# Down projection of a pre-norm transformer layer: 2x2 block products with seven multiplications, weights cast in DRAM

## The reference

```python
x = x + attention(layernorm(x)) @ Wo + bo        # 32 heads, 8 KV heads, head size 64
h = layernorm(x)
Wg, Wu, Wd = ((w - 128) * scale[:, None] for w, scale in
              ((gate_w, gate_scale), (up_w, up_scale), (down_w, down_scale)))
y = silu(h @ Wg.T) * (h @ Wu.T)                  # 8192 wide
out = x + y @ Wd.T                               # back to 2048
```

## Time and profile before

| | us |
|---|---|
| median of 3 runs | 2027.4 (2023.74 to 2028.51) |
| the profiled execution, own time | 2026.54 |
| its span on the slowest core | 2025.0 |
| spans of the other cores | 2020.3 to 2024.1 |
| PE busy | 1975.2 (98% of the span) |
| DVE busy | 1038.9 (51%) |
| ACT busy | 1059.9 (52%) |
| POOL busy | 124.8 (6%) |
| DMA: POOL's queue | 134.23 MB, 38.8% of 16 engines' span |
| DMA: SP's queue | 77.98 MB, 12.9% |

### The profile page before, as it was taken

The page is one execution under the profiler, slowest core; times in us unless marked ns, Lnnn a source line. Parts: engine busy times, 40 slices in busy tenths (PEclk is TensorE's granted clock), DMA queues, the critical chain, the costliest instruction groups (busy, mean ns, idle before and its releaser), DMA issues.

```text
span 2025.0 us, 31971 instructions; the slowest of 8 cores (2020.3 to 2025.0 us)
## 1 busy us (share of the span) xinstructions
PE 1975.2 (98%) x11664; PEld 985.2 (49%) x11664; DVE 1038.9 (51%) x1425; ACT 1059.9 (52%) x1203; POOL 124.8 (6%) x177
## 2 busy tenths in 40 slices
PE   5999999999999999999999999999999999999999
PEld 3545555555555554444444444444444444444444
DVE  5624666666666667666666666666666102020202
ACT  2425889888888854544454444444544233223230
POOL 2000110110001100000000000000000000000000
PEclk9999999999999999999999999999999999999999
DMA  9628644442138348555555445544445857474651
GB/s 231 192 42 141 98 70 74 74 86 46 32 64 129 88 134 197 111 105 110 113 111 105 84 86 93 93 84 84 86 90 94 214 122 150 79 151 83 123 123 42
DMA packets 47382, 214.24 MB, mean 106 GB/s; under 512 B 5888, under 2 KB 5888, under 8 KB 30080
## 3 DMA queue, kind: packets, MB, share of 16 engines
q0 software_dynamic: 20160, 134.23, 38.8%
q1 hardware_dynamic: 27072, 77.98, 12.9%
HBM read 319.14 MB, written 27.26 MB: 171 GB/s over the span
## 4 chain that ended last, share of the span: by engine, by line
PE 93%; DMA 3%; DVE 2%; issue 1%; ACT 1%; DVEq 0%; ACTq 0%; POOLq 0%; SPq 0%
PE PS_B L166 22%; PE PS_D L166 20%; PE PS_C L166 20%; PE PS_A L166 19%; PE PS_D L162 4%; PE PS_B L162 3%; PE PS_C L162 2%; PE PS_A L162 2%; DMA arena<-wq 2%; DVE arena L200 1%; DMA arena<-wv 1%; PE PS_D L177 1%; DVE bns L200 1%; DVE arena L202 1%; DMA arena<-xt 0%
## 5 line engine op out<-in xcount | busy, mean ns | idle before, releaser
L166 PE MATMUL PS_D<-arena 128*128 128x256 bf16 (+1 forms) x2674 | 527.8, 320 | 14.3 <-DVE arena L200 11.2
L187 ACT ACTIVATE arena<-arena 128x1024 bf16<-128x1024 bf16 x384 | 379.9, 1048 | 289.2 <-DMA arena<-dwt 289.2
L166 PE MATMUL PS_B<-arena 128*128 128x512 bf16 (+1 forms) x2413 | 516.6, 357 | 0.2 <-DVE arena L200 0.2
L166 PE MATMUL PS_A<-arena 128*128 128x512 bf16 (+2 forms) x2175 | 458.8, 355 | 10.5 <-DMA arena<-wv 7.7
L166 PE MATMUL PS_C<-arena 128*128 128x512 bf16 (+1 forms) x2200 | 467.7, 354 | 0.8 <-ACT arena L187 0.8
L166 PEld LDWEIGHTS PS_B<-arena 128*128 128x128 bf16 (+1 forms) x2413 | 211.9, 97 | 259.7 <-issue 34.5
L187 ACT ACTIVATE arena<-PS_B 128x1024 bf16<-128x1024 f32 (+1 forms) x203 | 194.3, 957 | 265.8 <-PE PS_B L162 265.6
L166 PEld LDWEIGHTS PS_D<-arena 128*128 128x128 bf16 x2674 | 239.8, 98 | 177.0 <-issue 79.0
L200 DVE TENSOR_TENSOR arena<-arena 128x1024 bf16<-128x1024 bf16 (+2 forms) x500 | 301.8, 622 | 11.8 <-ACT arena L187 2.7
L200 DVE TENSOR_TENSOR arena<-PS_A,arena 128x512 f32<-128x512 f32 (+1 forms) x106 | 74.1, 699 | 455.0 <-PE PS_A L162 455.0
L166 PEld LDWEIGHTS PS_C<-arena 128*128 128x128 bf16 (+1 forms) x2200 | 190.8, 97 | 234.8 <-issue 34.3
(11 more groups left out here) (45 smaller groups left out, 893.7 us busy)
## 6 DMA issues: line engine op xcount, KB each, us to landing
arena<-gwt POOLq DMA_DIRECT2D x32, 1024.0 KB, 9.0
arena<-uwt POOLq DMA_DIRECT2D x32, 1024.0 KB, 9.0
arena<-dwt POOLq DMA_DIRECT2D x32, 1024.0 KB, 9.8
arena<-xt SPq DMA_DIRECT2D x16, 1024.0 KB, 13.3
arena<-wq POOLq DMA_DIRECT2D x32, 512.0 KB, 7.6
arena<-wo POOLq DMA_DIRECT2D x6, 2048.0 KB, 24.6
arena<-xt SPq DMA_DIRECT2D x32, 256.0 KB, 7.1
x2d<-arena SPq DMA_DIRECT2D x32, 256.0 KB, 6.5
```

Source lines behind the costliest of these rows:

```text
L166: e.matmul(o, ll, rr, start=a, stop=b, skip_group_check=k))
L187: e.activation(o, i, f, bias=b, scale=s)
```

## The change

The output is cut in halves `nu` of 1024 columns. In each half the product of y (8192 rows, 1024 tokens) with the weights is a 2x2 block product: the blocks of y are `isub` by `th`, the blocks of the weights are the same `isub` of the rows by the two 512-column parts of the half. Seven products take the place of eight, each summed in PSUM over the whole contraction in 16 steps of 512 rows. They are done in four slots `sl`, two at a time in two groups of four banks (`E`, `D`), the last one alone; a step `g` is one of 2 x 4 x 16. Two matmuls per bank and product make 8 matmuls for a product of a step.

- The int32 weights are cast to bf16 in DRAM (`dws`), by 32 DMAs of POOL that read 2 MB and write 1 MB each, one every eight attention steps.
- In the down projection SP loads pieces of 256 KB of `dws` (128 rows of 2 KB) into a ring of 13 buffers (`ring_loads`), in the order of use: 2, 3, 2 and 2 pieces per step in the four slots, 288 in all. The reloads of `hmd` are in the same queue, one ahead of each of the first twelve steps.
- `forms(g + 1)` stands ahead of step g on ACT and DVE: it centres pieces, combines two of them (128x1024), and combines two blocks of y for each product that needs it (two operations of 128x512 each). Buffers `WF` and `XF` alternate by step.
- `evict` empties a group of banks after each slot: on ACT and DVE into `T_` and `V_`, or with the scale into `X2P`. It stands behind `forms(g + 1)` and ahead of `forms(g + 2)`.
- x2d is loaded, the scale and stores are done by `later_ops`, of which one is taken at every even step: a load of 256 KB by POOL into one of two buffers `XL`, the addition on DVE, and a store by POOL.
- The last four steps of the last slot are done bank by bank.

```diff
-    dwt = nc.dram_tensor("dwt", [4, 8, P, 4096], I32, kind="ExternalInput")
+    dwt = nc.dram_tensor("dwt", [32, 512, 1024], I32, kind="ExternalInput")
...
+    dws = nc.dram_tensor("dws", [32, 512, 1024], BF16, kind="Internal")
...
+            if k < 256 and k % 8 == 1:
+                xd_dwc = g_dma("DWC", dws[k // 8, :, :], dwt[k // 8, :, :])
...
-            if i < 64:
-                src = (gwt if i % 2 == 0 else uwt)[i // 2, :, :]
-            else:
-                src = dwt[(i - 64) // 8, DGRP[(i - 64) % 8], :, :]
+            src = (gwt if i % 2 == 0 else uwt)[i // 2, :, :]
...
-                center(u + 2, q)
+                if u + 2 < 64:
+                    center(u + 2, q)
...
-            if u + 4 < 96:
+            if u + 4 < 64:
...
+        RG_KB = [190, 192, 194, 196, 98, 100, 102, 104, 114, 120, 130, 94, 96]
+        GRP_BANKS = {"E": [6, 7, 0, 1], "D": [2, 3, 4, 5]}
+        STEPS = list(range(6, 16)) + list(range(6))
...
+        PROD_X = {5: (11, 12, "add"), 1: (11, 22, "add"), 3: (11, 0, ""),
+                  7: (12, 22, "subtract"), 6: (21, 11, "subtract"),
+                  2: (21, 22, "add"), 4: (22, 0, "")}
+        SLOTS = [((("E", 5), ("D", 1)), (22, 11)),
+                 ((("E", 3), ("D", 7)), (12, 22, 21)),
+                 ((("E", 6), ("D", 2)), (11, 12)),
+                 ((("D", 4),), (21, 11))]
+        G = [(nu, sl, st) for nu in range(2) for sl in range(4) for st in range(16)]
...
+        def ring_loads(g):
+            while ring_n[0] < len(LOADS):
+                r = ring_n[0] % 13
+                if ring_n[0] >= 13 and LOADS[ring_n[0] - 13][0] > g:
+                    break
+                g2, qt = LOADS[ring_n[0]]
+                nu, sl, st = G[g2]
+                ring_n[0] += 1
+                for w in ring_free[r]:
+                    y_wait(*w)
+                b = (nu * 4 + WS[qt]) * 16 + STEPS[st]
+                ring_of[(g2, qt)] = r
+                ring_dma[(g2, qt)] = ("RG%d" % r, y_dma(
+                    "RG%d" % r, RG(r),
+                    dws[b // 4, (b % 4) * P:(b % 4 + 1) * P, :]))
...
+        def forms(g):
+            nu, sl, st = G[g]
+            prods, qts = SLOTS[sl]
+            e0 = 2 * (st % 2)
+            we = {}
+            for n, (grp, j) in enumerate(prods):
+                we[grp] = st % 4 if sl == 3 else e0 + n
+                wf_at[(g, grp)] = we[grp]
+            raw = {qt: RG(ring_of[(g, qt)]) for qt in qts}
...
+            elif sl == 2:
+                e, d = we["E"], we["D"]
+                a = ("ACT", cen(12, raw[12], -128.0))
+                b = ("ACT", cen(11, WF(d), -128.0, d))
+                wf_rdy[(g, "D")] = b
+                wf_rdy[(g, "E")] = comb(e, raw[12], WF(d), "add", [b])
+                fr = {11: b, 12: wf_rdy[(g, "E")]}
...
+            for n, (grp, j) in enumerate(prods):
+                a, b, op = PROD_X[j]
+                if not op:
+                    continue
+                e = e0 + n
+                xf_at[(g, grp)] = e
+                v_wait(*xf_busy[e])
+                v_hm(st)
+                for pl in range(2):
+                    p = 2 * STEPS[st] + pl
+                    xf_rdy[(g, grp)] = ("DVE", v_op(
+                        "tensor_tensor", XF(e)[:, pl * 512:(pl + 1) * 512],
+                        xhm(p, a // 10, a % 10), xhm(p, b // 10, b % 10),
+                        ALU_OF[op], inc=True))
...
+            tail = nu == 1 and sl == 3
+            if tail and st >= 12:
+                if st < 15:
+                    return
+                for i in range(4):
+                    for g2 in range(g - 3, g + 1):
+                        step_mm(g2, "D", 4, i, g2 == g, i == 0)
+                    pe_done[("D", i)] = ("PE", C['pe'])
+                return
+            for grp, j in SLOTS[sl][0]:
+                for i in range(4):
+                    step_mm(g, grp, j, i, i == 3 or st == 15, i == 0)
+                    pe_done[(grp, i)] = ("PE", C['pe'])
+                step_done(g, grp)
...
+        def add_x2(kind, i, view, tm, nu, n, tok):
+            e = xl_n[0] % 2
+            xl_n[0] += 1
+            g_wait(*xl_free.get(e, ("PE", pe_m[(63, 6)])))
+            c = nu * 1024 + n * 512
+            ld = ("XL%d" % e, g_dma("XL%d" % e, XL(e),
+                                    x2d[tm * P:(tm + 1) * P, c:c + 512]))
+            v_wait(*ld)
+            v_wait(*tok)
+            t = ("DVE", v_op("tensor_tensor", view, view, XL(e), ALU.add, inc=True))
+            xl_free[e] = t
+            return t
+        def x2_out(kind, i, view, tm, nu, n, tok):
+            def f():
+                t = add_x2(kind, i, view, tm, nu, n, tok)
+                out_store(kind, i, view, tm, nu, n, t)
...
+            elif sl == 2:
+                for i in range(4):
+                    v_tok[i] = vtt(V_(i), gb("E", i), V_(i), ALU.add,
+                                   [pe_done[("E", i)]])
+                    bank_free[("E", i)] = [v_tok[i]]
+                for i in range(4):
+                    v_tok[i] = vtt(V_(i), V_(i), gb("D", i), ALU.subtract,
+                                   [pe_done[("D", i)], v_tok[i]])
+                    t_tok[i] = vtt(T_(i), T_(i), gb("D", i), ALU.subtract, [])
+                    bank_free[("D", i)] = [t_tok[i]]
+                def tail(i):
+                    def f():
+                        v_tok[i] = scale(V_(i), i, 1, v_tok[i])
+                        x2_out("V", i, V_(i), 4 + i, nu, 1, v_tok[i])()
+                    def f2():
+                        t_tok[i] = scale(T_(i), i, 0, t_tok[i])
+                        t_tok[i] = add_x2("T", i, T_(i), i, nu, 0, t_tok[i])
+                    return [f, f2]
+                for i in range(4):
+                    later_ops.extend(tail(i))
...
+        y_wait("DWC", xd_dwc)
+        ring_loads(-1)
+        ds_load(0, 0)
+        ds_load(0, 1)
+        forms(0)
...
+        for g, (nu, sl, st) in enumerate(G):
+            if g < 12:
+                xd_hrl[g // 4] = y_dma("HRL%d" % (g // 4), blk(reload_kb[g], 2048),
+                                       hmd[g, :, :])
+            if g + 1 < len(G):
+                forms(g + 1)
+            ring_loads(g + 1)
+            step(g)
+            if later_ops and st % 2 == 0 and st < 15:
+                later_ops.pop(0)()
+            if st == 15:
+                evict(nu, sl)
+            if nu == 0 and sl == 3 and st == 15:
+                ds_load(1, 0)
+                ds_load(1, 1)
...
-        for c in range(32):
-            q, cc = divmod(c, 8)
-            grp = DGRP[cc]
-            i = 64 + c
-            t_wait(ACT, act_cen[i])
-            if q == 0 and cc >= 5:
-                t_wait("HRL%d" % (cc - 5), xd_hrl[cc - 5])
-            if q == 0 and cc < 5:
-                t_wait(DVE, dve_hm[(4 * grp + 3, 22)])
-            for tm in range(8):
-                if cc == 0:
-                    if q == 0:
-                        t_wait(DVE, dve_t22[62 if tm < 3 else 63])
-                    else:
-                        t_wait(DVE, dve_ev[(q - 1, tm)])
-                for k in range(8):
-                    pr, isub = 4 * grp + k // 2, k % 2
-                    mm(BK(tm), HM(pr, isub, tm // 4)[:, (tm % 4) * P:
-                                                     (tm % 4 + 1) * P],
-                       RAW(i)[:, k * 512:(k + 1) * 512],
-                       start=(cc == 0 and k == 0), stop=(cc == 7 and k == 7),
-                       inc=(k == 7))
```

More of the change, by code:

```diff
@@ new lines, in build_program, with step_mm @@
+        bank_free = {}
+        for g_ in ("E", "D"):
+            for i_, b_ in enumerate(GRP_BANKS[g_]):
+                bank_free[(g_, i_)] = [("DVE", dve_t22[62 if b_ < 3 else 63])] \
+                    if b_ < 6 else []
+        first = {("E", 5), ("D", 1), ("D", 2)}
+        pe_done = {}
+        def step_mm(g, grp, j, i, last, wait):
+            nu, sl, st = G[g]
+            if wait:
+                t_wait(*wf_rdy[(g, grp)])
+                if (g, grp) in xf_at:
+                    t_wait(*xf_rdy[(g, grp)])
+                elif STEPS[st] < 6:
+                    t_wait("HRL%d" % (STEPS[st] // 2), xd_hrl[STEPS[st] // 2])
+                else:
+                    t_wait(DVE, dve_hm[(2 * STEPS[st] + 1, 22)])
+            if st == 0:
+                for w in bank_free[(grp, i)]:
+                    t_wait(*w)
+            x = PROD_X[j]
+            for pl in range(2):
+                if (g, grp) in xf_at:
+                    l = XF(xf_at[(g, grp)])[:, pl * 512 + i * P:
+                                            pl * 512 + (i + 1) * P]
+                else:
+                    l = xhm(2 * STEPS[st] + pl, x[0] // 10,
+                            x[0] % 10)[:, i * P:(i + 1) * P]
+                new = (grp, j) in first
+                mm(gb(grp, i), l, WF(wf_at[(g, grp)])[:, pl * 512:(pl + 1) * 512],
+                   start=(new and st == 0 and pl == 0), stop=(st == 15 and pl == 1),
```

(31 more changed lines are left out.)

193 lines of the change are left out of this document (140 added, 53 removed).

## The result

The change makes the kernel slower: the median is 2114.8 us, the ratio to before 1.041, 95% interval 1.038 to 1.044. 2022.8 was forecast, in a range of 2002 to 2044. Medians in this document count every execution, also the few in which the cores of one die run at a lower granted clock throughout (here one of four, 2416.2 us), and the ratios leave those out. The other three took 2099.1, 2112.3 and 2117.4 us. The one at 2099.1, the quickest, is the profiled one, with a span of 2097.6 on core 6; the other cores took 2073.0 to 2096.4.

What follows compares the result with a forecast made beforehand. PE was taken to bound the kernel throughout. Removed matmuls save 55.3 us, waits and clock give 50.7 back, so 4.6 us less: 2021.9 against the profiled 2026.5, given as 2022.8 for the median, range 2002 to 2044.

Steps and rivals of the forecast that it cites:

- The saving: Down projection: 256 of 2048 matmuls removed at 0.216 us each, 55.3 us less, all on the path.
- The start: Start of down: step 0 needs a combined y block from DVE, so PE starts 3.5 us late.
- The entry into slot four: After slot three: twelve evictions, then DVE work, put the first x2d addition's end 7.5 us into the slot.
- the forecast's own list: Signs expected in the changed profile, among them DVE's x2d waits as largest new wait and no PE waits for weight pieces.
- The first slot of the second half: Down, after the first fourth slot: PE waits of 4.3, 4.4 and 4.1 us, plus 1.7 us of lower clock.
- The casts in attention ... I count 0: Attention: casts hidden beside PE at 5.7 us of the engines, one every 17 us; cost 0, bounds 0 and some 6 us.
- The rival for this (10%): Attention: casts over 8 us or blocking the queue make `wq` late, above all for first tiles; 8 to 15 us more; 10%.
- L + 4.3 us: Fourth slots: a round of four steps, paced by x2d loads, takes 8.7 us where PE needs 6.9.
- L: Time from issue to landing of an x2d load in down: 4.4 us taken, own range 3.9 to 5.0.
- The rival of long landings: Fourth slots: queues share 10.8 us of engine work per round, landings take 5.0 to 7.0 us, kernel slower; 24%.
- the rule that I set beside it: Down: DVE work keeps POOL from writing DMA descriptors, so x2d loads land later; 18 us more, 2041.
- the clock: Down: PE's clock falls after standing still, twice, at 1.7 us lost each; 3.4 us.

Runs made afterwards that it cites:

- experiment 1: The kernel before, with the 32 casts added in attention and their results unused: 2079.8 us, ratio 1.019.
- experiment 4: The changed kernel with the 32 casts moved from attention into gate and up, the last three issues double: 2091.8 us, ratio 1.029.
- kernel 6: The kernel of experiment 5 with each x2d load issued one addition earlier, ahead of the store that waits for DVE: 2028.6 us, ratio 0.9997.
- experiment 10: The kernel before, with twelve pauses of PE in down, each waiting for three otherwise unneeded DVE operations: 2066.6 us, ratio 1.019.
- experiment 2: The changed kernel with only the first of 32 casts, all pieces read from its block, so the output is wrong: 2115.6 us, ratio 1.033.
- experiment 5: The changed kernel with ten casts in attention and 22 in gate and up: 2075.1 us in the single comparable execution, no ratio.
- (3): The changed kernel with the rows of `dws` padded, so casts go in 2 KB rows instead of 32 KB: 2109.4 us, ratio 1.039.

## Why the prediction was wrong

**Right.** The saving: 256 matmuls fewer and PE at 0.216 us where nothing holds it. The start: PE waited 3.2 us, 3.5 was forecast. The entry into slot four (7.1, forecast 7.5). That x2d would be the largest new wait of DVE in down, and that it would set the pace of slot four. By the forecast's own list these were the marks to look for, and they were there. PE itself had no wait for pieces of weights, and a piece took 0.86 us of the engines (11.70 MB in 76.7% of 50 us, 1690 to 1740), 0.96 was put. The first slot of the second half agrees by luck: 15.7 us over the ideal, 14.5 forecast, but it is 10.6 of waits where 12.8 were put and 5.1 of lower clock where 1.7 were.

**Wrong: "The casts in attention ... I count 0".** It was 46.3 us on the slowest core, and 16 to 63 in experiment 1. Two steps of it failed. First the price: the row of a load from DRAM into SBUF, 5.7 us of the engines, stood for a cast from DRAM to DRAM, which costs 10.1 (experiment 4). One in every 17 us is then 0.6 of the engines, where 0.31 were taken already. "If a cast costs twice as much" stood in the text, as a bound of 6 us once, but it was put down at one place only, the first `wq` loads. Second, the place: I looked for the cast in the queue of the casts, at the first `wq` loads. `wq` was late through the whole stage (6.2 to 16.8 us), and so was `xt`, of another queue (4.4 to 16.9), and behind `xt` POOL's own additions, which hold back `wq` and DVE: 22 waits, 328.8 us, where before there were 8 with 66.1. POOL appeared in the text as an issuer of DMAs, and its additions stand in the very order rows that front the change. The rival for this (10%) came nearest, with "or blocks the queue for that long", but named `wq` alone and priced it above all for the first tiles, at 8 to 15 us.

**Wrong: the round of slot four, "L + 4.3 us" with L = 4.4.** The form of the sum was right: 13.2 us with a landing of 10.7, 13.1 with 8.6, 11.9 with 7.3, so round minus landing is 2.5 to 4.6 where 4.3 was put. The size of L was wrong. It was taken from loads that had the DMA engines nearly to themselves, at a share of 0.31. In slot four the engines are busy for 0.78 of the time with weights, x2d and stores, and all of them land late together: DMA of 1807 to 1857 us,

```profile
arena<-dws SPq DMA_DIRECT2D x31, 256.0 KB, 5.7
arena<-x2d POOLq DMA_DIRECT2D x7, 256.0 KB, 8.1
```

where a piece of weights took 3.3 us from 1690 to 1740. The rival of long landings had said so, with 10.8 us of DMA work in a round, but stopped at L = 7; the three landings in the rounds have a mean of 8.9, the one behind them 6.2. Three rounds of 12.7 instead of 8.7 make 12.1 us more; the entry took 0.4 less and the last part of the slot 6.1 instead of 3.2. Together that is the 14.6 of the table; the 10.7 of slot four and the end is put down to the same wait, though its rounds were not taken apart. As SP's transfers are late in the same measure as POOL's, 3.3 to 5.7 against 4.7 (1750 to 1800) to 8.1, the rows speak for shared engines more than for the rule that I set beside it, by which DVE's work would hold POOL's descriptors (the Trainium skill, "SBUF — State Buffer", section "SBUF: two separate sides"). In kernel 6's slot four SP's pieces land in 9.3 us, later than POOL's x2d with 8.4. No run separates the two entirely.

**Half right: the clock.** 3.4 us were forecast, and PE is busy for 26.3 us longer than its matmuls take at 0.216. By the starts of the matmuls, 21.9 us of this are matmuls at a lower clock. 11.5 lie in the two fourth slots, where PE waits for x2d anyway (the row below: 124 matmuls are 26.8 us of work, in 33.8 of busy time at clock 0.83), so that they may cost little by themselves. The other 10.4 are 2.9 in the first slot, 1.2 in each third one, and 5.1 in the first slot of the second half: three times the forecast's 3.4. What was mis-sized is how much of it there is; a pause after which the clock fell cost 2.0 us in experiment 10, 1.7 was put.

```profile
1807.00:1857.00 50.00, 33.79 (x124) 13.17 (x123) 20.85 (x36) 5.12 (x6) 6.07 (x12) 0.83 0.78 225
```

**The account.** The profiled executions differ by 72.6 us: 46.3 ahead of down, which experiments 1 and 2 put down to the casts, and 26.3 in down. The forecast of down was -4.6, so it missed by 30.9: 14.6 in the first fourth slot, 10.7 in the second and the end, and 5.6 elsewhere, where the clock cost 7.0 more than forecast and the waits somewhat less. The sum of the two, against a range that ended at 2044, is why the result lies outside it: the range took each cause to its bound, but not both at once, and the bound of the casts was that of a single place. With the casts spread out (experiment 5) the miss that remains lies in the fourth slots and the slot behind the first of them, where x2d is waited for, and with x2d loaded ahead the kernel stands at 2028.6. That this is inside the forecast's range confirms nothing, as it is another kernel than the one forecast.

**Open.** Why reading one block repeatedly is slower (experiment 2); why down is slower still with short rows (3) and with the casts spread (5); and how much of a landing in slot four is the sharing of engines and how much the queue of POOL.

## What to carry to other kernels

Before work is put on an idle engine or queue, ask not only whether its own stage has room, but whose short transfers share its 16 engines, and what waits in order behind those: here a cast in POOL's queue made SP's `xt` late, and POOL's additions, which waited 22 times for it, carried that on to DVE and PE. Take the landing time of a transfer from a stretch that is as full as the new one will be, not from the quietest row of the same size. A load that is issued behind a store which waits for the last load has its whole landing in the loop; issuing it one round earlier made down 29 to 49 us shorter here, core by core.

## What was unexpected

- A cast from DRAM to DRAM, 2 MB in and 1 MB out in 32 KB rows, takes 10.1 us of the 16 DMA engines; into SBUF the same sizes take 5.7.
- Beside such casts a 256 KB load of another queue lands in 16.9 us instead of 4.4; with the cast in 2 KB rows, at the same share of the engines, in 9.6.
- All pieces read from one block of 1 MB: down 477 to 522 us, against 470 to 476 from 32 blocks.
- Of twelve pauses of PE of 2.8 us, three were followed by matmuls at a lower clock, at 2.0 us each, and nine by none.
